# Every product of a Toeplitz convolution issued as four matmuls, one for each 32-column strip of the array

## The reference, cut to what matters

```python
x = x + L0(x)   # long convolution: y = irfft(rfft(x, 2L) * rfft(K, 2L))[:L] + D * x, then a length mask
x = x + L1(x)   # per sequence one of 16 matrices 1024x1024: einsum('bsi,boi->bso', x, w)
x = x + L2(x)   # the same with other matrices
x = x + L3(x)   # gated feed-forward layer (1024 -> 2752 -> 1024) with low-rank additions per sequence
```

## Time and profile before

| | us |
|---|---|
| median of 3 runs | 2053.85 |
| lowest, highest of them | 2049.83, 2056.23 |
| the profiled execution, its own time | 2051.15 |
| its span, from first to last instruction | 2049.5 |

### The profile page before, as it was taken

How to read it: one execution, slowest core, us unless ns; L and a number is a source line. 1 busy time by engine, 2 the same in 40 slices (tenths; PEclk the granted TensorE clock), 3 DMA queues, 4 the chain that set the end, 5 groups by cost and what they waited for, 6 DMA issues and landing times.

```text
span 2049.5 us, 34188 instructions
## 1 busy us (share of the span) xinstructions
PE 2003.6 (98%) x10048; PEld 1701.1 (83%) x10048; DVE 1771.9 (86%) x2240; ACT 1007.3 (49%) x1259; POOL 145.0 (7%) x241
## 2 busy tenths in 40 slices
PE   4999999999999999999999999999999999999998
PEld 3999888888888788888888888888888888888887
DVE  7897999999999988888887779989888888868787
ACT  2223888888886543343443434464343443434332
POOL 3200000000003222210000020000000000000000
PEclk9999999999999999999999999999999999999999
DMA  7997999999998667754344996645344344478565
GB/s 282 372 343 295 356 347 354 363 350 361 347 361 329 178 184 210 209 166 123 107 118 145 337 303 212 211 149 143 109 123 120 107 119 113 118 240 303 194 203 190
DMA packets 263681, 471.07 MB, mean 230 GB/s; under 512 B 115462, under 2 KB 119750, under 8 KB 243910
## 3 DMA queue, kind: packets, MB, share of 16 engines
q1 hardware_dynamic: 246498, 427.58, 61.4%
q0 software_dynamic: 14944, 42.50, 6.7%
q10 hardware_dynamic: 2180, 0.26, 0.1%
HBM read 430.10 MB, written 63.73 MB: 241 GB/s over the span
## 4 chain that ended last, share of the span: by engine, by line
PE 85%; DVE 7%; DMA 4%; issue 2%; ACT 1%; DVEq 1%; ACTq 0%; SPq 0%
PE ps L2514 20%; PE ps L2516 19%; PE ps L2515 19%; PE ps L2376 6%; PE ps L2421 5%; PE ps L2423 5%; PE ps L2422 5%; DMA W<-in_w 3%; PE ps L2610 3%; DVE part L1708 1%; PE ps L2430 1%; PE ps L2650 1%; PE ps L2649 1%; DVE rows L1819 1%; ACT part L964 1%
## 5 line engine op out<-in xcount | busy, mean ns | idle before, releaser
L2514 PE MATMUL ps<-rows,oph 128*128 128x512 f32 x1196 | 468.4, 392 | 2.4 <-DVE opl L1819 1.6
L2516 PE MATMUL ps<-rows,opl 128*128 128x512 f32 x1196 | 466.1, 390 | 0.0
L2515 PE MATMUL ps<-rows,oph 128*128 128x512 f32 x1196 | 465.7, 389 | 0.0
L1708 DVE TENSOR_TENSOR part<-W,part 128x2048 fp32r<-128x2048 f32 x152 | 343.0, 2285 | 10.4 <-ACT part L964 9.8
L1822 DVE TENSOR_TENSOR tmp<-ps,tmp 128x512 f32<-128x512 f32 (+2 forms) x344 | 242.7, 706 | 101.8 <-PE ps L2516 53.1
L964 ACT ACTIVATE part<-W 128x2048 fp32r<-128x2048 f32 x152 | 290.9, 1916 | 78.4 <-DMA W<-in_w 56.6
L2516 PEld LDWEIGHTS ps<-rows,opl 128*128 128x128 f32 x1196 | 224.5, 188 | 49.2
L2514 PEld LDWEIGHTS ps<-rows,oph 128*128 128x128 f32 x1196 | 225.3, 188 | 44.3 <-DVE opl L1819 3.6
L2515 PEld LDWEIGHTS ps<-rows,oph 128*128 128x128 f32 x1196 | 224.8, 188 | 40.6
L2514 PE MATMUL ps<-th,wdh 128*128 128x512 f32 (+1 forms) x656 | 249.4, 380 | 2.3 <-DVE tmp L1822 1.2
L2515 PE MATMUL ps<-tl,wdh 128*128 128x512 f32 (+1 forms) x656 | 248.6, 379 | 0.0
(11 more groups left out here) (284 smaller groups left out, 2951.0 us busy)
## 6 DMA issues: line engine op xcount, KB each, us to landing
W<-in_w SPq DMA_DIRECT2D x152, 1024.0 KB, 6.8
raw<-in_wgu SPq DMA_DIRECT2D x168, 256.0 KB, 3.1
traw<-kept_acts SPq DMA_DIRECT2D x78, 512.0 KB, 5.0
wraw<-in_wd SPq DMA_DIRECT2D x70, 512.0 KB
toep<-kpad SPq DMA_DIRECT2D x31, 1024.0 KB, 9.7
kept_acts<-tmp SPq DMA_DIRECT2D x84, 256.0 KB, 2.4
lraw<-picked_b SPq DMA_DIRECT2D x176, 96.0 KB, 2.1
lraw<-picked_b SPq DMA_DIRECT2D x176, 64.0 KB, 1.8
```

Of the source, the lines that this page charges most:

```text
L1708: V.tensor_tensor(out=wl[c][:], in0=W[:, c], in1=wh[c][:].bitcast(F32), op=ALU.subtract).then_inc(w_lo, 1)
L2514: mm(to, lhsT=wh, rhs=mh, start=start, stop=False)
L2515: mm(to, lhsT=wh, rhs=ml, start=False, stop=False)
L2516: return mm(to, lhsT=wl, rhs=mh, start=False, stop=stop)
```

## The change

Each product of the convolution, a 128x128 stationary operand against n moving columns, is written as four matmuls. Strip t takes stationary columns 32t to 32t+31 and writes PSUM partitions 32t to 32t+31; the moving operand, n columns on 128 partitions, is the same for all four. In the code's order the four strips of T(d) stand one after the other, then come those of T(d+1). The last matmul of each strip of a pair adds 1 to `conv_done` (or `last_parts`), so these count four for each pair (or part), and all waits on them are multiplied by four. `kernels`, the loads, VectorE's work, the buffers and the layers behind are as before.

```diff
--- before.py
+++ after.py
@@ -68,6 +68,8 @@
 GATHERED = SEQ * 3 * 16
 TURN = 4
 LAST_BANKS = (3, 4, 5)
+STRIPS = 4
+SW = P // STRIPS
 CHUNK_LINKS = 11
 assert HALF == P // 2 and ROWS_AT == (B + SPARE) * LT * H * 4
 
@@ -493,7 +495,7 @@
             def reload(c, k):
 
                 q = c * PAIRS + k
-                sp.wait_ge(conv_done, q - (RING - 1))
+                sp.wait_ge(conv_done, q * STRIPS - (RING - 1) * STRIPS)
                 if k == PAIRS:
                     sp.wait_ge(k_out, c * 16 + 32)
                 load_toeplitz(q, k % RING)
@@ -875,7 +877,7 @@
             for s in range(SEQ // 2, SEQ):
                 gather_inner(0, s, slice(0, SPLIT))
             for s in range(SEQ):
-                pool.wait_ge(conv_done, 2 * s + 1)
+                pool.wait_ge(conv_done, (2 * s + 1) * STRIPS)
                 gather_outer(0, s, slice(0, SPLIT))
 
 
@@ -1474,7 +1476,7 @@
             def add_conv(c, i):
 
                 q = c * PAIRS + i
-                dve.wait_ge(conv_done, q + 1)
+                dve.wait_ge(conv_done, q * STRIPS + STRIPS)
                 mi = masked[:, i % 2].rearrange("p e l b -> p e (l b)")
                 V.tensor_tensor(out=mi, in0=bank(i % RING).rearrange("p (e w) -> p e w", e=2),
                                 in1=lmask[:].rearrange("p l b -> p (l b)").unsqueeze(1)
@@ -1726,9 +1728,9 @@
                 chan = (NCHUNK - 1) * CH + 2 * i
                 for n, (e, first, end) in enumerate(((0, 0, LT), (1, 0, WK), (1, WK, LT))):
                     if first:
-                        dve.wait_ge(conv_done, H // TG)
+                        dve.wait_ge(conv_done, H // TG * STRIPS)
                     else:
-                        dve.wait_ge(last_parts, n + 1)
+                        dve.wait_ge(last_parts, (n + 1) * STRIPS)
                     done = ps[:, LAST_BANKS[n], 0:LT * B].rearrange("p (l b) -> p l b", l=LT)[:, first:end]
                     V.tensor_tensor(out=masked[:, i % 2, e, first:end], in0=done, in1=lmask[:, first:end],
                                     op=ALU.mult).then_inc(part_masked, 1)
@@ -2373,10 +2375,13 @@
                     rows = urev[:, i % RING, e].rearrange("p l b -> p (l b)")
                     for d in range(LT):
                         n = (LT - d) * B
-                        last = mm(ps[:, i % RING, (e + 1) * LT * B - n:(e + 1) * LT * B],
-                                  lhsT=toep[:, i % RING, e, d * P:(d + 1) * P], rhs=rows[:, 0:n],
-                                  start=d == 0, stop=d == LT - 1)
-                last.then_inc(conv_done, 1)
+                        for t in range(STRIPS):
+                            strip = slice(t * SW, (t + 1) * SW)
+                            last = mm(ps[strip, i % RING, (e + 1) * LT * B - n:(e + 1) * LT * B],
+                                      lhsT=toep[:, i % RING, e, d * P + t * SW:d * P + (t + 1) * SW],
+                                      rhs=rows[:, 0:n], start=d == 0, stop=d == LT - 1)
+                            if e == TG - 1 and d == LT - 1:
+                                last.then_inc(conv_done, 1)
 
             kernels(0)
             convolve(0, 0, first=True)
@@ -2395,12 +2400,15 @@
                 pe.wait_ge(conv_free, c * PAIRS + (i + 1))
                 for n, (e, first, end) in enumerate(((0, 0, LT), (1, 0, WK), (1, WK, LT))):
                     rows = urev[:, i % RING, e].rearrange("p l b -> p (l b)")
-                    to = ps[:, LAST_BANKS[n], 0:LT * B]
                     for d in range(end):
                         l = max(first, d)
-                        last = mm(to[:, l * B:end * B], lhsT=toep[:, i % RING, e, d * P:(d + 1) * P],
-                                  rhs=rows[:, (l - d) * B:(end - d) * B], start=d == 0, stop=d == end - 1)
-                    last.then_inc(conv_done if first else last_parts, 1)
+                        for t in range(STRIPS):
+                            strip = slice(t * SW, (t + 1) * SW)
+                            last = mm(ps[strip, LAST_BANKS[n], l * B:end * B],
+                                      lhsT=toep[:, i % RING, e, d * P + t * SW:d * P + (t + 1) * SW],
+                                      rhs=rows[:, (l - d) * B:(end - d) * B], start=d == 0, stop=d == end - 1)
+                            if d == end - 1:
+                                last.then_inc(conv_done if first else last_parts, 1)
 
             for c in range(NCHUNK - AHEAD, NCHUNK):
                 for i in range(PAIRS):
```

## The result

The changed kernel takes 2064.19 us (median, 2060.93 to 2068.18) against 2053.85; the ratio is 1.0055, with a 95% interval of 1.0045 to 1.0064. It is slower, by 10 us, where the forecast had 108 us and a range from 2130 us up.

The account below looks back on a forecast made before the run. It took TensorE to bound the convolution: 108.6 us for channels, 3.3 for the last pair, less 3.8 covered, gave 108.1 on 2051.15; with the median 2.7 us above that execution, 2162 us. Range 2130 to 2420 us, at 0.81.

Parts of the forecast that it names:

- A half's interval T(n): Convolution: each float32 product runs as two halves, each streaming n columns in 0.833 n + 2 ns, with a load-bound floor.
- the 112 ns load goes: Convolution rival: short loads of different strips also run side by side, a channel takes 1956 ns, 2038 us; chance 0.06.
- Step 7: Picked layers behind the convolution: a longer convolution hides none of their wait for W, so nothing is given back.
- step 5: Convolution's semaphores: 3 more increments per pair and 9 in the last, between 0 and 3.2 us, taken as 0.
- step 2: Convolution's matmul order: strips start like stairs, a channel takes 4072 ns instead of 2320, +108.6 us; chance 0.50.
- own sign of being wrong: Convolution: the forecast is wrong if a product of 256 columns takes under 0.6 or over 1.2 us.
- Step 4: A slower convolution covers pair 0's Toeplitz wait and the waits of `kernels` for VectorE within the first chunk: -3.8 us.
- Step 1: Convolution's instructions: each product becomes four matmuls, eight halves, each streaming the same columns; total streaming is fourfold.
- Faster: Convolution rival: strips overlap in load and stream, VectorE then binds, at most -15.9 us, 2038 us; chance 0.06.
- All four strips at once: Convolution rival: all strips stream together with load as before per column, 2402 ns a channel, 2059 us; chance 0.10.
- The clock falls: Convolution rival: matmuls filling a quarter of the array drop to 1.2 GHz, every T doubles, about 2412 us; chance 0.05.
- both cases in which strips run side by side: Convolution rivals: all four strips at once, 2052 to 2075 us, chance 0.10; and faster, 2038 us, chance 0.06.

Follow-up runs that it names:

- e8: Changed kernel with two halves per product instead of four strips, plus unused products ahead of the third and the loop's filter products; 2048.32 us, 0.9974 of the kernel before.
- e4: Changed kernel with three unused 256-column products ahead of the filter product in each loop pass; 2063.47 us, 1.0055 of the kernel before.
- e6: Changed kernel with Toeplitz loads from pair 4 on bringing only 128 of 1024 columns, output wrong; 2053.1 us in one execution.
- e5: Changed kernel with two halves of 64 stationary columns per product instead of four strips, everywhere; 2046.99 us, 0.9963 of the kernel before.
- e9: The two-halves kernel of e5 measured again, on the chip of e8; 2048.18 us, 0.9969 of the kernel before.

## Why the prediction was wrong

**What held.** A half's interval T(n) = 0.833 n + 2 ns holds for strips too (0.22 us between starts at 256). The strips overlap. A channel of 1956 ns, the price of the rival "the 112 ns load goes", was measured as 1.97 us. Step 7 held: what follows the convolution takes 2049.5 - 188.24 = 1861.3 us before and 2062.6 - 201.75 = 1860.9 after. No run sets the price of the increments (step 5) apart.

**What failed, first: step 2.** It had "if matmuls start in the order written, as all in the trace do, the first half of strip t + 1 starts only once the second half of strip t has". The trace of before had only one stream, and in it no order could be seen to be kept between strips. All four first halves start within 0.03 us, and a strip runs ahead of another. The forecast's own sign of being wrong came true: a product of 256 columns, two intervals, takes 0.43 us, under its 0.6. The step's +108.6 us should have been -20.5 (62 x 0.33) of TensorE's time. Step 4 fell with it: the waits of `kernels` for VectorE weren't covered but grew from 24.5 to 31.2 us. The Trainium skill's "TensorE: Matmul & The Clock Gate" (Part 3: Packing small matmuls), with matmuls that start and end strictly in order, differs from the rows at 196.65 us above, and the measurement decides.

**What failed, second: a term that the sum lacked.** Step 1 counted four times the matmuls and asked only what they stream, not how they reach the engine. The unrolled code has to be brought in 16 KB packets through transfer queues that the earlier trace rows show full. Before, a packet lasted four pairs, 18.6 us, and came in time; with strips it lasts 4 us. The pauses sum to 17.8 us; with light transfers, where they are 2.0, the profiled execution shows a gain of 2.8 us in place of the loss of 13.5.

**Third, the rivals.** "Faster" had the right product and the right next bound (VectorE), but bounded the gain by VectorE's 15.9 us of waiting. Of that, 9.7 us lie behind the last filter product, where the loads of `u` bind next (the tail of the halves is 36.4 and 35.8 us, 1.6 and 2.2 under that of before), and 4.0 us are waits for pair 0 in the loop, in a cycle with the filter product. So the best run, e8, has the picked layers start only 5.7 us earlier. "All four strips at once" at 2059 us came nearest in time (2052 to 2075 holds the measured 2064), by luck: it kept the loads one after the other, and had no pauses. "The clock falls" was right that it can, wrong in why: it fell for a while in or behind waits of 1.7 to 3.0 us, not because strips fill a quarter of the array. In e4 it stays at 1.00 under strips in passes 2 to 5.

The range failed because it left out, at 0.16, both cases in which strips run side by side, on the strength of an order that no row showed.

## What to carry to other kernels

Splitting the stationary operand by columns shortens loads and streams side by side, so for float32 products of under some 130 columns, bound by a 112 ns load, it cuts TensorE's own work by 14% in this stage, of which other bounds left under 6 us of time here; two halves give nearly as much as four strips (2.02 against 1.97 us). Count the instructions as bytes as well: unrolled code is brought through the same queues as the data, and a stage that fills them may not take four times the matmuls. Keep to one form, since going between forms costs what it gains, and ask what the next engine's own cycle leaves to win before pricing a faster product.

## What the runs showed of the hardware

- Column strips don't wait for each other: four loads and four matmuls start 7 ns apart, and a strip can be in the next pair while others still have matmuls of the last one to start.
- Code is brought in packets of 16 KB, 256 bytes for a float32 matmul (12 packets for 768 matmuls). Where new code ran under dense transfers (240 to 410 GB/s in the pauses themselves), TensorE stood still for 0.3 to 3.7 us after 256 or 512 instructions, and for at most 0.26 in the tail of e6, with light ones. A loop of 16 KB x 4 pays only in its first pass.
- A change between products of 128 and of 32 columns and back costs 0.33 us.
- The granted clock went to the 1.2 GHz level for some 3.4 us in or behind waits of 1.6 to 4.5 us in some executions, and in others of the same kernel not (e5 once, e9 never; e9 has waits of 1.5 to 3.4 us).
